# Token lists in DRAM with 32-byte entries in place of 4-byte entries, in a three-stage Perceiver layer kernel

## The reference

```python
x = x + cross_attention(layernorm(x), ctx, Wq, Wk, Wv, Wr, ...)      # keys go through cos
x = x + causal_top8_attention(layernorm(x), W_q, W_k, gain, bias, ...)
# third stage: a mixture of 8 experts, one expert for each token
h = layernorm(x)                       # 2048 tokens
router_probs = softmax(h @ Wr)         # 8 experts
e, p = argmax(router_probs), max(router_probs)
x = x + p * (gelu(h @ W1[e] + b1[e]) @ W2[e] + b2[e])    # W1: 256 x 1024, W2: 1024 x 256
```

## Time and profile before

| what | us |
|---|---|
| median of 3 runs | 520.58 |
| lowest, highest | 519.25, 527.82 |
| the profiled execution, its own time | 522.69 |
| its span in the trace | 520.6 |

### The profile page before, as it was taken

One profiled execution on the slowest core, in us unless ns is written; L12 is line 12 of the kernel. 1 busy time (PEld: TensorE's weight loads), 2 busy tenths in 40 slices (PEclk: granted clock), 3 DMA queues, 4 the chain that ended last, 5 costly groups with the idle time before them and its releaser, 6 DMA issues. The chain is left out here.

```text
span 520.6 us, 10379 instructions
## 1 busy us (share of the span) xinstructions
PE 456.7 (88%) x2839; PEld 336.9 (65%) x2840; DVE 286.1 (55%) x904; ACT 268.8 (52%) x587; POOL 186.8 (36%) x326
## 2 busy tenths in 40 slices
PE   4889999999999759999999167985977999999992
PEld 3545565666666426666665055885967899999992
DVE  1556778888898548898898334763321121222220
ACT  2366768877788527788777233534213132233320
POOL 2732235334653414653545043442231332223210
PEclk9799999999999969999999768899999899999997
DMA  8612522325415305415551090353549556555300
GB/s 229 206 39 93 171 92 64 110 93 173 132 44 171 91 1 171 132 43 170 171 174 42 0 362 22 99 207 118 146 124 373 150 203 212 206 178 171 125 0 1
DMA packets 49106, 69.13 MB, mean 133 GB/s; under 512 B 8702, under 2 KB 38976, under 8 KB 48932
## 3 DMA queue, kind: packets, MB, share of 16 engines
q1 hardware_dynamic: 42820, 59.12, 34.6%
q0 software_dynamic: 3520, 8.23, 4.6%
q10 hardware_dynamic: 2720, 1.26, 0.9%
HBM read 62.20 MB, written 7.30 MB: 133 GB/s over the span
## 5 line engine op out<-in xcount | busy, mean ns | idle before, releaser
L1311 PE MATMUL pK<-stage,Wkr 128*128 128x512 f32 x256 | 126.2, 619 | 9.8 <-DVE stage L739 9.2
L1154 ACT ACTIVATE XF<-pT,b_now 128x128 f32<-128x128 f32 x184 | 52.6, 368 | 119.3 <-PE pT L1334 82.3
L1334 PE MATMUL pT<-XF,stage 128*128 128x128 f32 x736 | 92.0, 285 | 4.5 <-DMA stage<-in_L_ffn_W_dram 4.5
L1334 PEld LDWEIGHTS pT<-XF,stage 128*128 128x128 f32 x736 | 90.9, 201 | 6.9 <-issue 5.8
L1348 PE MATMUL pK<-W,XF 128*128 x368 | 87.0, 387 | 2.9 <-issue 1.3
L1348 PEld LDWEIGHTS pK<-W,XF 128*128 128x128 f32 x368 | 68.7, 193 | 12.6 <-issue 3.9
L1311 PEld LDWEIGHTS pK<-stage,Wkr 128*128 128x128 f32 x256 | 45.3, 196 | 48.7 <-issue 48.2
L356 POOL TENSOR_SCALAR ve<-mv 128x1 f32<-128x1 f32 x48 | 13.3, 276 | 157.2 <-DVE mv L662 157.1
L1135 ACT ACTIVATE stage<-pK,bkr 128x512 f32<-128x512 f32 x64 | 42.9, 689 | 34.5 <-PE pK L1311 33.0
L1142 ACT ACTIVATE stage<-stage 128x512 f32<-128x512 f32 x64 | 40.5, 633 | 20.4 <-DVE stage L734 20.2
L734 DVE TENSOR_TENSOR stage<-stage 128x512 f32<-128x512 f32 x64 | 47.7, 746 | 1.2
(11 more groups left out here) (194 smaller groups left out, 696.2 us busy)
## 6 DMA issues: line engine op xcount, KB each, us to landing
stage<-in_L_ffn_W_dram SPq DMA_DIRECT2D x23, 1024.0 KB
stage<-in_ctx_dram SPq DMA_DIRECT2D x32, 512.0 KB, 4.9
W<-in_L_ffn_W_dram SPq DMA_DIRECT2D x8, 1024.0 KB, 5.9
rows_by_token<-rows_out SPq DMA_DIRECT2D x16, 256.5 KB
ctx_last<-in_ctx_dram SPq DMA_DIRECT2D x64, 32.0 KB, 4.0
X<-in_x_dram SPq DMA_DIRECT2D x1, 1792.0 KB, 7.5
stage<-in_L_ffn_b_dram SPq DMA_DIRECT2D x1, 1024.0 KB, 9.0
token_i<-tokens_by_expert SPq DMA_DIRECT2D x23, 0.5 KB
```

The costliest lines, as they stand in the source:

```text
L1154: ins = act.activation(f_hT[b][:, n * P:(n + 1) * P], pT[i][:, (n % 4) * P:(n % 4 + 1) * P], ACT.Gelu, bias=b1_now[:, b, n:n + 1])
L1311: mm = pe.matmul(pK[r][:], Wkr[:, c, r * P:(r + 1) * P], ctx_T[:, c, half * 512:(half + 1) * 512], start=c == 0, stop=c == DC - 1)
L1334: mm = pe.matmul(pT[i][:, (n % 4) * P:(n % 4 + 1) * P], W1[q][:, c, n * P:(n + 1) * P], f_inT[:, q % 2, c * P:(c + 1) * P], start=c == 0, ...
```

## The change

Each entry of `by_expert` becomes eight int32, all of them the token's number: 32 bytes. The constant `ENTRY` is 8. The fill, the copy ahead of the scatter, the scatter and the load of a block's numbers move eight times the bytes; the gather and the store read their indices from the first of the eight. The fill's source tile is 128 x 144 int32, written by a memset, and each of the two fill DMAs reads it four times over, so that it moves 512 pieces of 576 bytes in place of 128 pieces of 288 bytes.

```diff
+ENTRY = 8
-        by_expert = nc.dram_tensor("tokens_by_expert", [(E + 1) * TOK, 1], I32, kind="Internal").ap()
+        by_expert = nc.dram_tensor("tokens_by_expert", [(E + 1) * TOK, ENTRY], I32, kind="Internal").ap()
-        token_now = sb("token_now", [P, 4], I32)
-        no_token = sb("no_token", [P, (E + 1) * TOK // P // 2], I32)
-        token_i = sb("token_i", [P, NBLK], I32)
+        token_now = sb("token_now", [P, 4, ENTRY], I32)
+        no_token = sb("no_token", [P, (E + 1) * TOK * ENTRY // P // 8], I32)
+        token_i = sb("token_i", [P, NBLK, ENTRY], I32)
...
-            made(pool.iota(no_token[:], [[0, (E + 1) * TOK // P // 2]], base=TOK, channel_multiplier=0))
-            half_list = (E + 1) * TOK // 2
+            made(pool.memset(no_token[:], TOK))
+            half_list, part = (E + 1) * TOK // 2, (E + 1) * TOK * ENTRY // P // 8
             for i in range(2):
-                pool.dma_start(by_expert[i * half_list:(i + 1) * half_list, :].rearrange("(p n) o -> p (n o)", p=P),
-                               no_token[:, 0:half_list // P]).then_inc(tokens_st[i], 16)
+                pool.dma_start(by_expert[i * half_list:(i + 1) * half_list, :].rearrange("(p r n) o -> p r (n o)", p=P, r=4),
+                               no_token[:].rearrange("p (r n) -> p r n", r=1).to_broadcast([P, 4, part])
+                               ).then_inc(tokens_st[i], 16)
...
-                pool.tensor_copy(token_now[:, r0:r0 + 2], token_all[:, bass.ds(2 * q, 2)]).then_inc(S["token_r"], 1)
+                pool.tensor_copy(token_now[:, r0:r0 + 2, :], token_all[:, bass.ds(2 * q, 2)].rearrange("p (g o) -> p g o", o=1
+                                                                                             ).to_broadcast([P, 2, ENTRY])).then_inc(S["token_r"], 1)
...
-                                            token_now[:, r0 + i:r0 + i + 1], None).then_inc(tokens_st[s], 16)
+                                            token_now[:, r0 + i, :], None).then_inc(tokens_st[s], 16)
...
-                                        bass.IndirectOffsetOnAxis(ap=token_i[:, j:j + 1], axis=0)
+                                        bass.IndirectOffsetOnAxis(ap=token_i[:, j, 0:1], axis=0)
...
-                pool.indirect_dma_start(out_v, bass.IndirectOffsetOnAxis(ap=token_i[:, j:j + 1], axis=0),
+                pool.indirect_dma_start(out_v, bass.IndirectOffsetOnAxis(ap=token_i[:, j, 0:1], axis=0),
...
-                    sp.dma_start(token_i[:, j:j + 1], by_expert[bass.ds(r, P), :]).then_inc(token_ld[j % SLOTS], 16)
+                    sp.dma_start(token_i[:, j, :], by_expert[bass.ds(r, P), :]).then_inc(token_ld[j % SLOTS], 16)
```

## The result

| | before | changed |
|---|---|---|
| median of 4 runs each, us | 522.17 | 499.95 |
| ratio, with its 95% interval | | 0.960 (0.951 to 0.969) |
| profiled execution, its own time | 522.69 | 497.54 |
| its span | 520.6 | 495.5 |

The kernel is 4% faster, by the whole of its interval. A second measurement of the same kernel with 6 runs gave 499.33 us and 0.958 (0.953 to 0.963). All ratios leave out the runs more than 1.5% above the fastest of their kernel: here 527.82 us of the kernel before (its median is 520.58 without it), 504.54 of the second measurement, and in the experiment with 4 bytes in a slot one of 595.53 us at a granted clock of 0.746. The gain between the medians of the runs that the ratio uses is 20.6 us, while the two profiled executions lie 25.1 us apart: that of the changed kernel is the fastest of its four.

What follows compares the result with a forecast made beforehand. TensorE was taken as the bound, with 63.9 us of gaps in 520.6. Terms -7.5 - 6.7 - 1.8 - 5.2 - 6.8 + 1.0 = -27.0 took 522.69 to 495.7; forecast 495 us, range 485 to 513.

Steps and rivals of the forecast that it cites:

- The landing: Time from a scatter's issue until its 128 writes land in DRAM: 3.0 us with 32-byte entries, against up to 10.5.
- Rival A: The scatter's landing doesn't shorten, small DRAM writes being slow whatever their size; only the fill counts, 522 us; chance 0.16.
- Rival B: The landing shortens by about half, to 6.5 us, neighbours still queueing at one place of memory; 510 to 512 us; chance 0.10.
- Term 1, wave 0: TensorE's 10.80 us gap before 301.08, waiting for `h`: earlier token numbers cut it to 3.3, -7.5 us.
- Term 2, the jump: The 9.22 us gap at the loop's jump back shrinks to some 2.5, -6.7 us; slow clock after it goes, -1.8.
- The least certain term: At the loop's jump back: an instruction fetch's completion stands behind the scatter's writes; otherwise -6.7 and -1.8 us don't come.
- rival C: Landing shortens, but the jump keeps its 9.2 us gap and wave 3 half of its gaps; 505.5 us; chance 0.10.
- Term 3, wave 2: The 3.46 us gap before 363.54 goes, -3.5, and the slow clock after it, -1.7; together -5.2 us.
- Term 4, wave 3: TensorE's 6.8 us of gaps between 383 and 406 go, `gather(7)` and block 7's W1 load being ahead; -6.8 us.
- The fill: GpSimd's issue of the two fill DMAs at the start grows fourfold, 1.39 to 5.6 us, partly covered; +1.0 us.
- rival D: The fill's issue goes by bytes, making GpSimd 9.7 us later at the start; slower, 530.1 us; chance 0.04.

Runs made afterwards that it cites:

- the spaced 4-byte run: Changed kernel with its 32-byte slots, but each scatter writes only 4 of a slot's 32 bytes; 502.27 us, ratio 0.962.
- the packed writes: Changed kernel plus two scatters of 128 packed 4-byte entries into an unread tensor, right ahead of the loop's jump back; 504.79 us, ratio 0.970.
- the run with the packed writes elsewhere: Changed kernel plus two scatters of 128 packed 4-byte entries into an unread tensor, in the loop's first pair, away from the jump; 499.66 us, ratio 0.960.

## Why the prediction was right, and where it was not

Forecast 495 us (485 to 513), measured 499.95. Forecast gain 27.0 us between profiled executions, measured 25.1 there and 20.6 in the medians of the runs that the ratio uses. The terms below are checked in the profiled executions.

- **The landing**, taken as 3.0 us between 2.1 and 10.5: right, 2.4 at the median. The reason given (entries share 32 bytes) is the one that the spaced 4-byte run shows. The 3.3 us taken as a landing of the 2052-byte rows was not one: it is a wait of SyncE that doesn't begin at their issue. Rival A, from the rule of the Trainium skill ("DMA: Bandwidth & Descriptors", section "Specifications") that under 512 bytes the DMA engine reads, modifies and writes, is out as a price here: 128 writes of 32 bytes, or even of 4 bytes apart, land like 128 of 1 KB. The 32-byte rule of the Trainium skill, "Collectives: The Full Stack", section "Rules for kernel authors", agrees for 32 bytes, but doesn't say that a 4-byte write alone in its 32 bytes is as quick. Rival B, a half-shortened landing, is out too.
- **Term 1, wave 0**, -7.5: measured -8.7, less 1.7 given back at the W1 wait. The step "the 2.19 us before 304.96 stay" failed by that 1.7: TensorE had block 0's rows 0.4 us sooner relative to the load's issue, and the load itself was 1.3 us longer on its way, 6.6 us from its issue to the product in place of 5.3. Why it was longer is open; with the same code there it took between 5.3 (entries of 64 bytes) and 7.3 us (the changed kernel's second profile).
- **Term 2, the jump**, -6.7 and -1.8: measured -7.8 in all. The gap is 1.86 us where 2.5 was expected; the prediction's own figures give 1.9 (landing at 177.7, 1.97 us for the fetch, 0.83 us for the copy, and TensorE idle since 178.57). The part for the slow clock, 1.8 us, was mis-sized: only 0.4 came (3.34 us for the four matmuls against 3.78). It would not have come at the full clock either. In the second profile of the changed kernel the four took 1.98 us, and TensorE then waited 2.21 us for `h` in place of 0.76: the next step waits for VectorE and not for the matmuls. The least certain term was right in cause, as far as the packed writes show it, and rival C lost on it.
- **Term 3, wave 2**, -5.2: this step failed. The numbers did come earlier, but I had named only the token wait of `gather(6)` and overlooked the one that its code puts first, for the landing of `store(2)`. The account of the kernel gave that wait from block 7 on; the code has it from `gather(4)` on. In the kernel before, the store had landed by the time that the numbers came; with these early, the store is late next: issued at 340.48, it holds `gather(6)` until 346.61, beside the W1 loads. The gap shrank by 0.95 us in place of 3.46. Of the 1.7 us for the slow clock nothing came: the 16 matmuls behind the gap took 3.07 us in place of 3.65, but the eight behind these 2.55 in place of 1.89, and from the last rank to the next block's rows it is 5.32 us before and 5.35 after. The run with `gather(6)` moved behind the counting shows this: the gap is gone, and the time 3 us lower.
- **Term 4, wave 3**, -6.8: under-sized. From the last rank to the end 10.1 us were gained. The 6.8 us of idle time went whole. Of the other 3.3 us about half is slow clock that I had not summed, at 404.82 us of the kernel before (16 matmuls in 5.27 us there, 3.62 in every block of the steady part); the rest lies in the same blocks, around their short gaps, and isn't broken down here.
- **The fill**, +1.0, bounds 0 to 9.7: over-sized. GpSimd's issue of the two DMAs took

```profile
15.90 1.76 POOL L392 DMA_DIRECT2D tokens_by_expert<-no_token  x2 [0.31 <-POOL no_token L389]
```

  against 1.39: +0.37 us for four times the pieces and eight times the bytes, in place of the +4.2 that counting pieces gave, so rival D is out. The +1.2 us that the changed kernel lost by 178 us is not the fill's: TensorE's first matmul starts 0.5 us later (7.02 against 6.53 us) and its products with `Wkr` at line 1288 (1291 in the changed kernel) 1.4 us later (15.26 against 13.90), both ahead of the fill at 15.90, and the run with the packed writes elsewhere, which has the same fill, starts its first context projection at 18.54 us, as the kernel before does at 18.51.

Term 3 promised 3.7 us more than came, and term 4 3.3 us less. That these cancel is luck, and it is why the sum came closer than its parts.

## What to carry to other kernels

When small indexed writes go to DRAM, count how many of them fall into the same 32 bytes, not how many bytes they move: give each its own 32 bytes, even if only 4 are written. A slow small write can cost more than its own waiters: here it also held up an engine behind a jump, by all that the traces show through the completion of an instruction fetch. When a wait is shortened, list every wait of the instruction behind it, from the code, and find the one that ends second: it is the new bound.

## What the runs showed of the hardware that was not expected

- The cost of packed writes grows with sharing: 2.4 us at the median alone in 32 bytes, 2.6 for 4 bytes alone, 3.7 with two sharers, 7.1 for 128 consecutive entries (eight sharers) in a tensor of their own, and 10.28 in the lists of the kernel before, where two such scatters come 1.4 us apart and can write into the same pieces.
- GpSimd's issue time hardly depends on the pieces of a direct DMA: 1.39 us for 256 pieces, 1.76 for 1024 and 2.04 for 2048 (entries of 64 bytes). The bytes don't show: 1024 pieces of half the size, with entries of 16 bytes, took 1.76 as well.
- Packed writes delay engines that have nothing to do with them, at a jump: 5.1 us for 256 writes of 4 bytes that no other engine waits for. Behind a jump VectorE goes on 2.1 to 2.5 us after an instruction packet of 8 KB has moved where no slow writes stand ahead of it, and 5.9 or 9.5 us after it where they do.
